# Attention layer with power-4 scores: the sum of relu scores of two full units added by GpSimd before TensorE streams it

## What is computed

```python
s = einsum('bhtd,bhsd->bhts', q, k)
s = s - s.mean(axis=-1, keepdims=True)
mad = abs(s).mean(axis=-1, keepdims=True) + 1e-06
s = s / mad * score_gain
s = where(causal, s, -1000.0)
r = maximum(s, 0.0) ** 4
att = r / (r.sum(axis=-1, keepdims=True) + 1e-06)
y = einsum('bhts,bhsd->bhtd', att, v)
```

## Time and profile before

| | |
|---|---|
| median of three runs | 805.56 us (805.55, 805.56 and 853.74) |
| the profiled execution, its own time | 808.65 us |
| its span, first to last instruction | 806.9 us |
| PE, DVE, ACT, POOL busy | 735.7, 671.1, 675.7, 513.7 us |
| units 36 to 167 (quads 3 to 13) | 517.2 us of the span |

### The profile page before, as it was taken

The page is one execution under the profiler, slowest core; times in us unless marked ns, Lnnn a source line. Parts: engine busy times, 40 slices in busy tenths (PEclk is TensorE's granted clock), DMA queues, the critical chain, the costliest instruction groups (busy, mean ns, idle before and its releaser), DMA issues.

```text
span 806.9 us, 17975 instructions
## 1 busy us (share of the span) xinstructions
PE 735.7 (91%) x5850; PEld 336.0 (42%) x5853; DVE 671.1 (83%) x1866; ACT 675.7 (84%) x1527; POOL 513.7 (64%) x537
## 2 busy tenths in 40 slices
PE   7978888889999999999999999999999999999886
PEld 6622121214444445444444444444444445443224
DVE  7679999998978887887888879788877988888883
ACT  4768989898888897988889898888989888898880
POOL 4015666745867667595766759576675957669690
PEclk9986889999999999999999999999999999999899
DMA  8865122274514542351334335133422623321395
GB/s 249 287 211 211 38 72 61 76 203 104 119 53 132 137 113 54 102 140 45 104 107 121 108 108 137 40 108 104 114 78 85 170 82 95 97 58 30 78 141 129
DMA packets 58350, 90.87 MB, mean 113 GB/s; under 512 B 8960, under 2 KB 41344, under 8 KB 58256
## 3 DMA queue, kind: packets, MB, share of 16 engines
q1 hardware_dynamic: 43200, 75.21, 33.7%
q0 software_dynamic: 10784, 12.53, 7.0%
q10 hardware_dynamic: 4272, 1.98, 0.8%
HBM read 61.29 MB, written 28.06 MB: 111 GB/s over the span
## 4 chain that ended last, share of the span: by engine, by line
PE 45%; DVE 24%; ACT 13%; issue 10%; POOL 7%; DMA 1%; DVEq 0%; ACTq 0%; SPq 0%; POOLq 0%
PE bank L983 17%; DVE W L1329 12%; PE bank L1018 7%; DVE junk_V L1321 6%; PE bank L998 6%; PE bank L1059 4%; ACT U L835 4%; POOL W L681 4%; ACT junk_A L827 3%; PE bank L1023 3%; PE bank L1068 3%; ACT W L856 2%; DVE W L1333 2%; PE bank L907 1%; ACT U L838 1%
## 5 line engine op out<-in xcount | busy, mean ns | idle before, releaser
L1329 DVE SCALAR_TENSOR_TENSOR W<-bank,U 128x512 f32<-128x512 f32 (+1 forms) x512 | 300.6, 649 | 21.4 <-ACT U L835 19.6
L983 PE MATMUL bank<-W,VS 128*10 128x512 f32 (+3 forms) x1536 | 297.5, 508 | 13.2 <-ACT W L856 9.0
L983 PE MATMUL bank<-U,usel 128*10 128x512 f32 (+3 forms) x1536 | 294.0, 506 | 0.0
L835 ACT ACTIVATE U<-bank 128x512 f32<-128x512 f32 (+1 forms) x512 | 253.9, 599 | 19.7 <-PE bank L1068 18.3
L1321 DVE TENSOR_SCALAR_CACHE_REDUCE junk_V<-bank 128x512 bf16<-128x512 f32 (+3 forms) x445 | 218.4, 533 | 55.7 <-PE bank L1059 54.9
L681 POOL TENSOR_TENSOR W<-W 128x1024 f32<-128x1024 f32 (+2 forms) x159 | 233.9, 1481 | 13.7 <-DVE W L1329 4.0
L670 POOL TENSOR_SCALAR_AFFINE_SELECT W<-W 128x512 f32<-128x512 f32 x127 | 83.0, 654 | 176.5 <-DVE W L1329 89.9
L856 ACT ACTIVATE W<-W 128x256 f32<-128x256 f32 (+2 forms) x225 | 192.2, 881 | 2.2 <-POOL W L670 1.2
L1068 PE MATMUL bank<-QS,KS 48*128 48x512 bf16 (+3 forms) x768 | 148.8, 334 | 19.8 <-DVE W L1329 12.9
L827 ACT ACTIVATE junk_A<-bank 128x512 bf16<-128x512 f32 (+3 forms) x195 | 88.2, 461 | 48.3 <-PE bank L1059 48.0
L1059 PE MATMUL bank<-KS,QS 48*128 48x512 bf16 (+3 forms) x640 | 98.8, 325 | 3.1 <-DVE parts L1265 1.7
(11 more groups left out here) (166 smaller groups left out, 673.2 us busy)
## 6 DMA issues: line engine op xcount, KB each, us to landing
wb<-in_experts SPq DMA_DIRECT2D x39, 707.0 KB, 5.5
qk_parts<-parts SPq DMA_DIRECT2D x8, 768.0 KB, 5.6
KS<-qk_parts SPq DMA_DIRECT2D x192, 32.0 KB
QS<-qk_parts SPq DMA_DIRECT2D x192, 32.0 KB
xt_all<-sorted_x SPq DMA_DIRECT2D x39, 130.0 KB, 5.9
sorted_x<-xt_all SPq DMA_DIRECT2D x3, 1300.0 KB, 12.0
xn_row<-weighted_y POOLq DMA_DIRECT2D x6, 512.0 KB, 7.1
v_stationary<-vb SPq DMA_DIRECT2D x4, 640.0 KB, 4.3
```

The lines of the kernel that those rows point to most:

```text
L835: act.activation(U[n % NU][:, g, 0:w], score(n, k), ACT.Relu).then_inc(u_ready, 1)
L983: last = pe.matmul(acc[32 * g:32 * g + VW, lo:HALF], usel[:, :] if of_u else VS[q % 2][:, j, :, g], (U if of_u else W)[n % NU][:, g, 0:HAL ...
L1329: vec.scalar_tensor_tensor(W[n % NU][:, g, 0:w], score(n, k), 0.0, U[n % NU][:, g, 0:w], ALU.max, ALU.mult).then_inc(w_done, 1)
```

## The change

In quads 3 to 13 the full units are taken in pairs, (4, 5) and (6, 7). POOL, after its squares of the second unit of a pair, adds the U of the first into the U of the second, in two instructions of 128x1024 elements. PE then leaves U out in `average` of units 4, 5, 6 and 7 and streams the sum of a pair once, in the `average` one unit later: that of 4 and 5 in unit 6, that of 6 and 7 in unit 8, behind unit 8's own. Waits are added for the sum (`u_added`), on PE ahead of that `average`, and on ACT where it writes the buffer of the pair's first unit again (units 8 and 10); ACT's wait on `used` is one unit stricter where the pair's second unit held the buffer (units 9 and 11).

`POOL_SQUARES` gives POOL one half of unit 7 and one of unit 8 where it had both of unit 7 and none of unit 8. `ROOM` lets the rows of experts be given back in masked units alone, one or two items in each.

```diff
--- before.py
+++ after.py
@@ -96,9 +96,11 @@
     HEADS = [(1, 0, 3, 2) if (PIECE_AT[n][-1][0] % 2 == 0) else (0, 1, 2, 3) for n in range(ALL)]
     SCATTERS = TOPK * NT
     PER_STEP = 2
-    POOL_SQUARES = [(1,), (1,), (1,), (1,), (0,), (0,), (0,), (0, 1), (), (1,), (1,), (1,)]
+    POOL_SQUARES = [(1,), (1,), (1,), (1,), (0,), (0,), (0,), (0,), (1,), (1,), (1,), (1,)]
     by_pool = lambda n, p: n * PER_STEP >= SCATTERS and p in POOL_SQUARES[n % NS]
     NU, AVLAG = 4, 2
+    PAIR_ENDS = [q * NS + k for q in range(EARLY, NQ - 2) for k in (5, 7)]
+    HELD = {b - i for b in PAIR_ENDS for i in range(2)}
 
 
     NXT, NWB, NYB = 6, 3, 4
@@ -115,7 +117,7 @@
 
 
     ROWS, BACK_AT, due = -1, [[] for _ in range(ALL)], []
-    ROOM = [1, 0, 0, 0, 2, 2, 2, 1, 2, 0, 0, 0]
+    ROOM = [1, 1, 2, 2, 0, 0, 0, 0, 1, 1, 2, 2]
     for n in range(ALL):
         due += [(p, m) for kind, p in FFN_AT[n - 1] if n and kind == "my" for m in [ROWS, *range(2 * len(tiles_of(p)))]]
         while due and len(BACK_AT[n]) < (ROOM[n % NS] if n < FFN_TO - 2 else 2):
@@ -268,7 +270,7 @@
         qk_in = [sem("quad_in0"), sem("quad_in1")]
         s_ready, u_ready, w_done, w_mask = sem("scores_ready"), sem("u_ready"), sem("w_done"), sem("w_masked")
         r_ready = [sem(f"r_ready{i}") for i in range(NU)]
-        used = sem("u_and_r_used")
+        used, u_added = sem("u_and_r_used"), sem("u_of_two_units_added")
         acc_ev = sem("acc_evacuated")
         y_out, s_out = [sem("y_stored0"), sem("y_stored1")], [sem("sums_stored0"), sem("sums_stored1")]
         p_ready, p_used = sem("piece_ready"), {"V": sem("piece_used_vec"), "A": sem("piece_used_act")}
@@ -679,6 +681,11 @@
                             pool.wait_ge(w_done, 4 * n + 2 * p + 2)
                         some = slot[:, 2 * p:2 * p + 2, 0:w]
                         pool.tensor_tensor(some, some, some, ALU.mult).then_inc(r_ready[n % NU], 1)
+                if n in PAIR_ENDS:
+                    pool.wait_ge(w_done, 4 * (n + 1))
+                    for p in range(2):
+                        to, more = (U[m % NU][:, 2 * p:2 * p + 2, :] for m in (n, n - 1))
+                        pool.tensor_tensor(to, to, more, ALU.add).then_inc(u_added, 1)
                 if n >= BIAS_FROM and (n - BIAS_FROM) % 2 == 0 and (n - BIAS_FROM) // 2 < B:
                     x_and_bias((n - BIAS_FROM) // 2)
                 for b in side(n, S_SUMS):
@@ -829,7 +836,9 @@
                                 at += w
                             last.then_inc(p_used["A"], 1)
                     w = HALF - LOW[n % NS]
-                    wait(act, used, n - NU + 1)
+                    wait(act, used, n - NU + 1 + (n - NU in PAIR_ENDS))
+                    if n - NU + 1 in PAIR_ENDS:
+                        act.wait_ge(u_added, 2 * (PAIR_ENDS.index(n - NU + 1) + 1))
                     for k, g in enumerate(HEADS[n]) if not NARROW[n % NS] else ():
                         act.wait_ge(s_ready, 4 * n + k + 1)
                         act.activation(U[n % NU][:, g, 0:w], score(n, k), ACT.Relu).then_inc(u_ready, 1)
@@ -976,15 +985,14 @@
             less(3, 0, 1)
 
 
-            def average(n, p, of_u):
+            def average(n, p, of_u, start=False, stop=False):
                 q, (c, j), lo = n // NS, STEPS[n % NS], LOW[n % NS]
                 for r in range(2):
                     g = 2 * p + r
                     last = pe.matmul(acc[32 * g:32 * g + VW, lo:HALF],
                                      usel[:, :] if of_u else VS[q % 2][:, j, :, g],
                                      (U if of_u else W)[n % NU][:, g, 0:HALF - lo],
-                                     start=(j == 0 and of_u == bool(p)), stop=(n % NS in ENDS and of_u != bool(p)),
-                                     skip_group_check=True)
+                                     start=start, stop=stop, skip_group_check=True)
                 return last
 
             def ffn(kind, k):
@@ -1088,10 +1096,19 @@
                     pe.wait_ge(r_ready[y % NU], 2 * (y // NU + 1))
                     if STEPS[y % NS][1] == 0:
                         wait(pe, acc_ev, y // NS * CH + STEPS[y % NS][0])
-                    average(y, 0, False)
-                    average(y, 1, True)
-                    average(y, 0, True)
-                    average(y, 1, False).then_inc(used, 1)
+                    first, end = STEPS[y % NS][1] == 0, y % NS in ENDS
+                    if y - 1 in PAIR_ENDS:
+                        pe.wait_ge(u_added, 2 * (PAIR_ENDS.index(y - 1) + 1))
+                    of_u = [u for u in (y, y - 1) if (u in PAIR_ENDS if u < y else u not in HELD)]
+                    average(y, 0, False, start=first)
+                    if of_u:
+                        average(of_u[0], 1, True, start=first)
+                        average(of_u[0], 0, True, stop=end)
+                    last = average(y, 1, False, start=first and not of_u, stop=end)
+                    for u in of_u[1:]:
+                        average(u, 0, True)
+                        last = average(u, 1, True)
+                    last.then_inc(used, 1)
                 if n == ALL:
                     experts_of_last()
```

## The result

| | before | changed |
|---|---|---|
| median | 805.55 us | 821.70 us (821.13 to 823.78, 4 runs) |
| ratio, 95% interval | | 1.0201 (1.0186 to 1.0215) |
| span of the profiled execution | 806.9 us | 822.0 us |
| units 36 to 167 (quads 3 to 13) | 517.2 us | 530.3 us |
| behind the last W | 20.8 us | 24.5 us |

The change made the kernel 2% slower: 16.1 us, where +2.8 was forecast. One of the four executions before (853.74 us) was in a slower state of the chip and does not count in the median. The profiled execution of the changed kernel is 2.1 us above its median, that of the kernel before 3.1 above its own; of the 15.1 us of longer span 13.1 lie in the eleven quads with pairs and 3.7 behind the last W, and the rest is 1.7 shorter.

What follows compares the result with a forecast made beforehand. PE was taken as first bound (91% busy), with all four engines at 90% or more in full units. -19.2 + 6.4 + 7.9 + 7.7 = +2.8 us on the 805.56 median gave 808.4 us, with 8 in 10 for 795 to 824.

Steps and rivals of the forecast that it cites:

- where 0.50 was put: Main forecast, 802 to 814 us: PE's gain is eaten by POOL and by the limit of the full units.
- the new wait: Rival: POOL's lag from full units passes 3.2 us and ACT stands at unit 8; 824 us, chance 0.19.
- PE's saving, -19.2 us: In `average`, each pair saves two waves of U products, 0.87 us; 44 waves in eleven quads, -19.2 us.
- What DVE and ACT leave of it, +6.4: Full units cannot shrink more than 1.17 us a quad because DVE is busy; +6.4 us against PE's saving.
- The addition's price: On POOL, each of 44 additions of 128x1024 takes 2.35 us, low end 1.94; 103 us in all.
- POOL's time, +7.9: POOL's work, idle gaps and additions exceed the length of some quads; what sticks out is +7.9 us.
- late masks, +7.7: Moved rows delay unit 82's mask; ACT's square waits 1.4 us, half taken, 0.7 a quad: +7.7 us.
- the hand-made run: POOL's queue followed through one profiled quad, units 76 to 82, with additions and moved work, at the old pace.
- The tables, 0: The square moved from unit 7 to unit 8 trades with ACT's, each engine keeping its count: no cost.
- Its signs: New wait's signs: ACT's U or PE's `average` released by the additions, full stretches of 16 us or more.
- POOL keeps up, 792.8 us: Rival: additions cost 1.94 us, only the DVE and ACT limit remains; 792.8 us, chance 0.24.
- The clock: Rival: PE's clock falls to 1.2 GHz in some full stretches; one in twenty gives 816 us; chance 0.04.

Runs made afterwards that it cites:

- experiment 2: Changed kernel with each of the 44 additions covering 16 columns of each head instead of 512, PE's work, waits and tables as changed: 795.08 us, ratio 0.9861.
- experiment 3: Changed kernel with additions and waits kept, but PE streams as many columns per unit as before the change: 822.01 us, ratio 1.0192.
- experiment 1: Changed kernel with no pairs: PE streams every U, POOL adds nothing, both tables (squares, rows given back) as changed: 808.91 us, ratio 1.0028.
- experiment 4: Changed kernel with each of the 44 additions on 256 of the 512 columns: 800.23 us, ratio 0.9921.
- experiment 7: Changed kernel with only the first pair of a quad (units 4 and 5), units 6 and 7 streamed as before: 805.82 us, ratio 0.9988.
- experiment 6: Changed kernel with POOL adding the second pair (6 and 7) behind mask and square of unit 8, PE waiting only before its products: 841.62 us, ratio 1.0424.

## Why the prediction was right or wrong

The time lies inside the range of 8 in 10 (795 to 824), near its upper end, but not where 0.50 was put (802 to 814); it falls in the stretch given to the new wait (815 to 832, 0.19), and got there another way. That the range held is owed to its width, not to the sum, which was wrong by 13 us. Whether the change costs more than 2%, which had 0.16, the interval (1.86 to 2.15%) leaves open. By step:

- **PE's saving, -19.2 us.** Right: 33 `average`s take 0.85 us less and 11 take 0.86 more, 18.6 us. U has 176 streams fewer (1536 to 1360). The sign that went with it, PE busy for some 19 us less, reads 6.7 in the changed kernel (491.4 to 484.6), where some products run at the lower clock, 15.9 in experiment 2, and 16.8 between experiment 3 and the changed kernel.
- **What DVE and ACT leave of it, +6.4.** Right in size (13.8 us measured in experiment 2, 12.8 forecast), wrong in place. The full stretch gained 0.25 us a quad (2.7 by 11); in experiment 2 most of the gain, 0.9 us a quad, lies in units 8 to 11. PE had run ahead in the full units and used its lead behind them.
- **The addition's price.** Right: 2.38 for 2.35 us.
- **POOL's time, +7.9, and late masks, +7.7, added to PE's -12.8.** This is the step that failed. Without PE's saving the additions cost 13.1 us (experiment 3 less experiment 1, 822.0 and 808.9), near the 15.6 of these two terms. With the saving they cost 26.6 (the changed kernel less experiment 2). The saving is worth 13.8 us while the additions are nearly free and nothing once they take their time, so the two parts could not be added up. I had PE waiting nowhere for POOL in the sum, although the hand-made run put the square of unit 80 at 368.9 against 368.83; and that run was at the old pace, with PE coming to unit 80 no sooner for what it saves. Measured, PE waits for the square of unit 8 for 2.9 us in the eleven quads without the saving and for 17.0 with it, once in every quad; ACT waits for masks for 12.7 and 29.9 us. I also bounded POOL by quad, as if its 9.4 us could be spread over 47: the added work is due within units 5 to 8, where POOL runs without a pause from the square of unit 77 to that of 80. The mask of unit 80 I had found 1.3 us later and charged nothing for; the 0.7 us a quad were for the mask of unit 82. The clock falls in four quads, up to 6.8 us, an estimate.
- **The tables, 0.** Wrong by 2 to 3 us (2.8 in experiment 1): nothing in the eleven quads, 3.4 behind the last W. I had looked at the moved square as a trade between two engines and not at what POOL has behind it in the last quad.
- **The rival of the new wait, 824 us.** Nearest in time. Its cause, a lag of POOL from the full units that is free up to a limit, fits experiments 2, 4 and 7. Its signs failed: the full stretches are 14.6 us and not 16 or more, the time is in the units behind, and neither ACT's U nor PE's `average` is released by an addition. ACT's wait for the sum appeared only in experiment 6, in unit 10. PE's `average` of unit 80, named beside it, is where PE stands.
- **POOL keeps up, 792.8 us.** What it would have given is experiment 2: 795.1.
- **Other signs.** The quads' mean is 48.2 us (46.5 to 48 was forecast), POOL's share 87% (near 90%), and ACT's squares wait for masks, as said.
- **The clock.** Held apart as a case of its own at 0.04, in the full stretches. It fell in four quads, each time in the masked units, and comes on top of the waits; what brings it down is not shown.

The estimate from the Trainium skill's figure (GPSIMD Engine Reference, section 3.1, 2.25 us an addition) was a little low: the trace has 2.38.

Open: how the 26.6 us divide between PE's pauses, ACT's late squares and the clock, what brings the clock down, and why the pairs of masked units gave nothing.

## What to carry to other kernels

Here work moved to an engine that looked 64% busy was free only until its lag reached the next deadline of the busy engines; find that deadline (here the square of the unit behind the added work), and price the work within the stretch up to it, not by the engine's share of the whole. Follow the queues at the new pace of the engine that is relieved, not at the old one: it comes to the deadline sooner. Do not add up the two halves of a trade: measured apart, the saving was worth 13.8 us, the added work cost 13.1 and the tables 2.8, which makes +2.1, and together they made +16.1. Measure the saving with the added work made tiny, then the added work at half and in full with the saving in place, and take the part whose price still fits; here one pair of two, and not in the first two quads.

## What the runs showed that was not expected

- The placement of about 6.6 indirect DMAs a quad, the same work in another order, was worth 72 us once POOL was near its limit (894.3 against 821.7), and nothing when it was not (experiment 1).
- A pause of PE of 4.42 us was followed by 1.2 GHz for the next `average`: 4.39 instead of 2.70 us. Pauses of some 2.1 us were followed by a fall once (567.2) and not another time (422.1), and two falls had no pause over 0.45 us in the 12 us ahead of them.
- With the additions at their full time the kernel takes 822.0 us without PE's saving and 821.7 with it; with the additions nearly free the same saving is worth 13.8 us.
- Half of the additions' columns cost nothing in eight of the eleven quads (365.6 us with 16 and with 256 columns), the other half 18.9 us.
